# A macaron block with delta-rule attention on one core: the plain chunk inverses are stored ahead of the copy that turns them

## The reference

```
x = x + 0.5 * ffn(layernorm(x))      # 256 -> 1024, gelu, -> 256
x = x + attn(layernorm(x))
x = x + 0.5 * ffn(layernorm(x))

# attn, for each of 4 heads of 64:
q, k, v = silu(short_conv(x @ Wq)), silu(short_conv(x @ Wk)), silu(short_conv(x @ Wv))
beta = sigmoid(x @ Wb)
# delta rule, in chunks of 32 tokens (q, k normalised; kb = k * beta):
A = -tril(kb @ k.T, -1)
T = solve_triangular(eye - A, eye, lower=True)      # inverse of a unit lower triangle
u, w = T @ (v * beta), T @ kb
u_i = u - w @ S ;  o_i = q @ S + tril(q @ k.T) @ u_i ;  S = S + k.T @ u_i
# then: four branches (two FIR filters of v, o, v) mixed by a gate, rmsnorm, @ Wo
```

## Time and profile before

| | us |
|---|---|
| timed runs, median (lowest, highest) | 1264.2 (1264.02, 1264.72) |
| profiled execution, span | 1267.5 |
| TensorE products busy (share) | 1090.1 (86%) |
| TensorE weight loads busy | 813.0 (64%) |
| VectorE busy | 836.8 (66%) |
| ScalarE busy | 547.8 (43%) |
| GpSimd busy | 410.0 (32%) |
| chain that ended last, by engine | TensorE 55%, VectorE 24%, ScalarE 8%, "issue" 5%, SP 3%, GpSimd 3%, DMA 1% |

### The profile page before, as it was taken

How to read it: one execution, slowest core, us unless ns; L and a number is a source line. 1 busy time by engine, 2 the same in 40 slices (tenths; PEclk the granted TensorE clock), 3 DMA queues, 4 the chain that set the end, 5 groups by cost and what they waited for, 6 DMA issues and landing times.

```text
span 1267.5 us, 25615 instructions
## 1 busy us (share of the span) xinstructions
PE 1090.1 (86%) x10348; PEld 813.0 (64%) x10348; DVE 836.8 (66%) x1556; ACT 547.8 (43%) x957; POOL 410.0 (32%) x640
## 2 busy tenths in 40 slices
PE   3778499789988999889988997899988998887738
PEld 2663387368854886378845894388746885477427
DVE  5754247686678857875677757785687757873363
ACT  1145125543375435643375327443474337531322
POOL 8005500482007610482019500581018400770000
PEclk9869679799999999999999999899999999995768
DMA  5031101402040201402040204101040204010000
GB/s 148 1 80 39 32 1 34 85 1 50 18 92 10 41 9 36 82 1 49 18 100 1 49 2 95 23 18 33 18 101 1 50 1 91 10 31 20 1 0 17
DMA packets 80245, 47.19 MB, mean 37 GB/s; under 512 B 55808, under 2 KB 73728, under 8 KB 80128
## 3 DMA queue, kind: packets, MB, share of 16 engines
q1 hardware_dynamic: 80128, 45.56, 16.0%
HBM read 30.86 MB, written 14.68 MB: 36 GB/s over the span
## 4 chain that ended last, share of the span: by engine, by line
PE 55%; DVE 24%; ACT 8%; issue 5%; SPq 3%; POOL 3%; DMA 1%; DVEq 0%; ACTq 0%; POOLq 0%
PE psum L774 11%; PE psum L776 9%; PE psum L775 9%; DVE conv_acc L1351 5%; PE psum L805 4%; DVE arena L1582 3%; PE psum L963 3%; PE psum L948 2%; PE psum L982 2%; PE psum L987 2%; SPq L346 2%; ACT arena L577 2%; DVE h_hi L1330 2%; PE psum L1140 2%; PE psum L903 2%
## 5 line engine op out<-in xcount | busy, mean ns | idle before, releaser
L515 POOL TENSOR_TENSOR l_prod<-arena 64x30 f32<-64x30 f32 (+14 forms) x240 | 151.5, 631 | 631.3 <-DMA arena<-l_dram 613.1
L573 ACT ACTIVATE h_f<-psum,b_col 128x512 f32<-128x512 f32 x128 | 88.0, 688 | 226.7 <-PE psum L776 205.6
L774 PE MATMUL psum<-w_hi,h_hi 128*128 128x256 f32 x512 | 153.1, 299 | 14.5 <-DVE h_lo L1331 14.4
L519 POOL TENSOR_TENSOR arena<-arena,l_prod 64x30 f32<-64x30 f32 (+14 forms) x240 | 157.2, 655 | 18.8
L776 PE MATMUL psum<-w_hi,h_lo 128*128 128x256 f32 x512 | 146.1, 285 | 0.0
L775 PE MATMUL psum<-w_lo,h_hi 128*128 128x256 f32 x512 | 146.1, 285 | 0.0
L1069 PE MATMUL psum<-v_shift,fir_w 128*32 128x512 f32 x1152 | 136.6, 615 | 3.4 <-DMA v_shift<-v_dram 3.4
L1351 DVE SCALAR_TENSOR_TENSOR conv_acc<-psum,conv_col,conv_acc 128x511 f32<-128x511 f32 x144 | 107.8, 748 | 35.1 <-ACT conv_acc L598 23.3
L1330 DVE CAST h_hi<-h_f 128x512 fp32r<-128x512 f32 x128 | 80.4, 628 | 66.5 <-ACT h_f L573 39.8
L774 PE MATMUL psum<-xt_hi,w_hi 128*128 128x512 f32 x256 | 110.2, 431 | 14.9 <-DVE b_half L1444 7.0
L774 PEld LDWEIGHTS psum<-w_hi,h_hi 128*128 128x128 f32 x512 | 98.9, 193 | 22.5 <-DVE h_lo L1331 18.2
(11 more groups left out here) (231 smaller groups left out, 2268.7 us busy)
## 6 DMA issues: line engine op xcount, KB each, us to landing
x_in<-in_L_attn_x SPq DMA_DIRECT2D x8, 512.0 KB, 4.0
v_dram<-v_fm SPq DMA_DIRECT2D x8, 512.0 KB, 2.8
v_shift<-v_dram SPq DMA_DIRECT2D x8, 512.0 KB, 4.9
out<-x_tok SPq DMA_DIRECT2D x8, 512.0 KB, 2.9
v_shift<-v_dram SPq DMA_DIRECT2D x8, 511.0 KB, 6.9
v_shift<-v_dram SPq DMA_DIRECT2D x8, 510.0 KB, 9.1
v_shift<-v_dram SPq DMA_DIRECT2D x8, 509.0 KB, 11.7
arena<-in_L_ffn_w SPq DMA_DIRECT2D x2, 1024.0 KB, 7.2
```

Of the source, the lines that this page charges most:

```text
L515: pool.tensor_tensor(prod, l_inv[:, k + 1:, k:k + 1].broadcast_to(shape), l_inv[:, k:k + 1, 0:k].broadcast_to(shape), ALU.mult).then_inc(i ...
L519: pool.tensor_tensor(l_inv[:, k + 1:, 0:k], l_inv[:, k + 1:, 0:k], prod, ALU.add).then_inc(inverted, 1)
L573: act.activation(h_f[:, m % 2, :], bank, ACT.Gelu, bias=b1_col[:, m:m + 1]).then_inc(read, 1)
L774: pe.matmul(dst, a_hi, b_hi, start=first, stop=False, **kw)
```

## The change

The store of the plain inverses now waits for 61 counts of `inverted`, which is the memset, and is issued ahead of the wait for the 62nd, the turning copy. The turned inverses are stored behind that wait, with a semaphore of their own, `tt_stored`. Of the loads the six into `t_low` are issued first, behind `t_stored` and `fir_done`, then the four into `x_t`, behind `tt_stored`. Nothing is changed on the other engines, and number, size and form of the DMAs stay as they are.

```diff
-        t_stored, t_loaded = sem("t_stored"), sem("t_loaded")
+        t_stored, tt_stored, t_loaded = sem("t_stored"), sem("tt_stored"), sem("t_loaded")
...
+                    sp.wait_ge(inverted, INV_STEPS * j + INV_STEPS - 1)
+                    sp.dma_start(t_dram.rearrange("c u i j -> (c u) i j"), l_inv[:, :, :]).then_inc(t_stored, 16)
                     sp.wait_ge(inverted, INV_STEPS * j + INV_STEPS)
-                    sp.dma_start(tt_dram.rearrange("c u j i -> (c u) j i"), l_turned[:, :, :]).then_inc(t_stored, 16)
-                    sp.dma_start(t_dram.rearrange("c u i j -> (c u) i j"), l_inv[:, :, :]).then_inc(t_stored, 16)
-                    sp.wait_ge(t_stored, 32 * j + 32)
-                    for c in range(CPT):
-                        sp.dma_start(x_t[32 * c:32 * c + 32, :, 32 * c:32 * c + 32],
-                                     tt_dram[c].rearrange("u j i -> j u i")).then_inc(t_loaded, 16)
+                    sp.dma_start(tt_dram.rearrange("c u j i -> (c u) j i"), l_turned[:, :, :]).then_inc(tt_stored, 16)
+                    sp.wait_ge(t_stored, 16 * j + 16)
                     sp.wait_ge(fir_done, j + 1)
                     for c in range(CPT - 1):
                         col = CHUNK * (c % 2)
                         for g in range(2):
                             sp.dma_start(t_low[32 * c:32 * c + 32, g, :, col:col + CHUNK],
                                          t_dram[c, 8 * g:8 * g + 8].rearrange("u i j -> i u j")).then_inc(t_loaded, 16)
+                    sp.wait_ge(tt_stored, 16 * j + 16)
+                    for c in range(CPT):
+                        sp.dma_start(x_t[32 * c:32 * c + 32, :, 32 * c:32 * c + 32],
+                                     tt_dram[c].rearrange("u j i -> j u i")).then_inc(t_loaded, 16)
```

## The result

The changed kernel is faster, by about twice what was forecast: 1254.06 us median (1247.41 to 1258.99, 20 runs) against 1262.53 (1255.3 to 1270.15, 20 runs) of the kernel before, ratio 0.9939, 95% interval 0.9919 to 0.9959. The forecast was 1260.3 with a range of 1256.0 to 1263.8, so the time lies outside, and the gain of 8.5 us stands against 3.9. Single runs of one kernel scatter over 12 to 15 us, which the three runs of before that were known ahead of the prediction (1264.0 to 1264.7) did not show; they lay 1.7 us above the median of twenty. Over all runs in which the mean clock is known too, 121 of the kernel before and 42 of the changed one, the means are 1261.8 and 1254.7 us: 7.1 us, standard error 0.7.

The account below looks back on a forecast made before the run. Two of eight merges, head and tail, were taken to wait for loads behind the stores. Gains of 2.55 and 1.33 us, 3.9 together, off 1264.2 gave 1260.3, range 1256.0 to 1263.8.

Parts of the forecast that it names:

- the two waits: TensorE waiting for loads at the head's and the tail's first merge product: gains of 2.55 and 1.33 us, 3.9 together.
- I take 3.6 and keep 2.9: Plain store's landing in the head: 3.6 us taken from the profile, 2.9 kept as the bound if alone on the queues.
- The estimate of 2.6: Landing of the 256 KB plain store by the skill's formula, 2.6 us; by it the forecast would be 1259.3.
- The tail: Entry of the last pass: loads land before VectorE ends, TensorE starts about 0.2 us behind VectorE, gaining 1.33 us.
- My forecast lets that moment move along with the work: TensorE's return to full clock, 17 us after work begins behind the head, was taken to shift with the work.
- Rival B: Behind the head, the clock returns earlier, behind the first filler: 5.4 us less, 1254.9 in all; chance 0.10.
- C: The tail's 1.54 us wait is not the loads, so only the head gains: 1261.6; chance 0.07.
- D: A refill of TensorE's code falls into a burst of loads, costing up to 8.1 us: 1268.4; chance 0.07.
- E: Store waits for something behind the memset, or issues and landing limit anyway; about 1.0 us gained: 1263.2; chance 0.06.
- A: Behind the head, the clock comes back later in the program, costing 2.7 us; net gain 1.2: 1263.0; chance 0.17.

Follow-up runs that it names:

- e1: Kernel before with the plain store ahead of the copy but the loads in the old order: 11.9 us from memset to the head's first merge product.
- e2: Kernel before with both stores behind the copy, the plain one first, and the loads in the new order: 12.5 us from memset to the head's first merge product.
- e7: Kernel before with the new order of stores and loads in the six body passes alone: ratio 0.9996 (0.9966 to 1.0025).
- e14: Kernel before with the new order in the head and the last pass, the old one in the six body passes: ratio 0.9966, mean 1256.7 us.
- e16: The kernel before, unchanged, run once more for a third trace; the kernel before against itself measured 1.0008 (0.9978 to 1.0038).
- e13: The changed kernel, run a third time: ratio to the kernel before 0.9979 (0.9948 to 1.0009), mean 1257.4 us.
- e9: Kernel before with 128 products that nobody reads (256 instructions with weight loads) ahead of the first merge's wait: ratio 0.9996 (0.9972 to 1.0021).
- e6: Kernel before with the new order of stores and loads in the last pass alone: ratio 0.9985 (0.9957 to 1.0013).
- e5: Kernel before with 45 products that nobody reads ahead of the first merge's wait: ratio 0.9972 (0.9942 to 1.0001).

## Why the prediction was wrong

*The mechanism of the two waits was right.* The early store took the copy off the chain, the swapped loads were needed for it (`e1`, `e2`), the two waiting merges gained and the six others did not (`e7`, `e14`), the tail's wait passed to VectorE, and the plain store, the ten issues and a last landing became the head's limit.

*"I take 3.6 and keep 2.9": mis-sized.* The plain store lands in 2.9. I took the row's duration with its circumstances, the other store half a microsecond ahead of it on the queue, though the change takes just that away; the turned store's 2.9 was the row to go by. The shorter landing is worth 0.7, but the ten issues took 0.2 longer and the last landing 0.1, so the head gained 3.04 instead of 2.55. The estimate of 2.6 by the Trainium skill's DMA: Bandwidth & Descriptors (Anatomy of one DMA) was nearer than the row, and still short of 2.88.

*The tail: 1.33 forecast, 1.0 to 2.2 measured.* The stretch from the memset falls from 13.2 or 13.3 to 12.0 and 12.3 in two traces and to 11.1 in the others. I had 11.95 from one trace. In that trace the clock fell to half for a moment just ahead of the merge (the slice 1136 to 1140 has 0.66), and VectorE's last step came late; behind a wait for loads this cost nothing. In the changed kernel VectorE ends the wait, and it counts. In the thirteen traces of the table VectorE's last step ends 10.8 us behind the memset's start in the six where the clock stood at full there, and 11.7 to 12.0 us in the six where it fell. That the fall is the cause is likely but not shown: in the thirteenth, `e16`, the step is late (12.1) without it. `e13`, with such a fall, starts as I computed (its chain of waits):

```profile
1128.49 0.03 DVEq L1343
1128.52 0.25 issue
1128.76 1.22 PE psum L877 x63
```

*"My forecast lets that moment move along with the work": the step that failed.* It held the return of the clock at 17 us behind the head's merge, and so the cost of half clock there at what one trace had. The clock's return is not tied to a step of the program but differs from one execution to the next, between 4 and 17 us behind the same product, and the first interval goes with it: 145.8 to 147.5 us where it is under 6, 150.0 to 152.1 where it is 10 or more. By the two profiles this is 5.2 of the 11.8 us; by the means over all runs it is less, as worked out below. My 17.2 was one draw. Rival B, at 0.10, gave its place and its size rightly (behind the first filler, 4.8 us after L875, and 5.4 us off; the changed kernel's trace has 4.9 and 5.2). I gave it as an effect of a shorter wait, which the traces don't bear out; a distribution would have been right.

How much of the mean is clock? Time at half clock, worked out from each run's span and mean clock (span x 2 x (1 - mean clock)), is 190.3 us for the kernel before and 183.2 for the changed one. Within either kernel a microsecond at half clock goes with 0.29 us of time. At equal half-clock time the changed kernel is 5.0 us faster (standard error 0.4), about what the stretches show, 3.0 in the head and 1.0 to 2.2 in the tail; the 7.1 us less at half clock are the other 2.0. Some 3 of these 7.1 are only the idle stretch grown shorter, in which half clock costs nothing, so that the split may as well be 5.9 and 1.2. The 0.29 is a correlation and not a price that an experiment showed: `e9` had 181 us at half clock and a mean of 1262.0, no faster than the kernel before (most of the time that it saved at half clock lies in the idle stretch, where it costs nothing).

With this the 6.2 us between the forecast, 1260.3, and the median, 1254.06, can be split roughly: 1.7 the reference (see there), 1.1 the two waits (5.0 instead of 3.9), 2.0 the lower half-clock time, and 1.4 what these twenty runs have over all runs (8.5 and 7.1).

*What stays open* is whether the new order makes an early return more likely. It was early in 5 of 6 traces with the new order in the head, in 1 of 5 with the old one, and in one of the two with half of the change (`e1`, `e2`). Chance can do that, and the set with `e13` had no less half clock with the new order. Keeping TensorE busy before the merge did not secure it. So the waits' part of the gain is shown, and the cause of the rest stays open.

*The reference.* The range was built around 1264.2, the median of three runs within 0.7 us. Twenty runs gave 1262.5 with a spread of 15. Around that, the same 3.9 us would have been 1258.6, still 4.5 above the result.

*The rivals.* C falls: the tail's "issue" was the loads, and `e6`, which changes nothing else, shortens that stretch from 13.3 to 11.1. D and E didn't come: the two stalls stayed where they were, and the store is issued 0.18 behind the memset's start. A, a later return, cannot be told from the draw. (Two bounds of the prediction differ: the store's and the load's give 1260.7, and the forecast's chance is put on a range up to 1260.9. Nothing hangs on it.)

## What to carry to other kernels

When a step is taken from between a producer and its DMA, walk the chain again with the landing that the transfer has alone, not with the one it had in company, and look for what hid behind the old wait and will now show. Read order changes by stretches between two fixed events in the trace, such as from the memset to the first product here, which repeat within 0.6 us where whole times scatter by 15. And before a forecast of a few microseconds, ask how far TensorE's clock differs from run to run: three agreeing runs don't tell.

## What the runs showed of the hardware

- Two stores of 256 KB on one queue, issued 0.5 us apart: the first lands in 2.9 us, the second in 3.6 to 3.7, whichever tensor it is.
- The same program got its full clock back 4.3, 16.9 or 17.2 us after the same product in three executions.
- Stalls of TensorE of 5 to 8 us without a releaser are waits for its code: each of the 38 in the 18 traces holds one 16 KB transfer of the `instruction` queue and ends 1.2 to 1.6 us after it. The two of the kernel before stand in bursts of long v_shift loads.
- Adding 60 or 90 instructions to TensorE's stream moved such stalls to other passes and made three of two, for example one interval from 151.7 to 137.5 and another from 139.0 to 144.9 us in `e5`; adding 256 left them in their passes.
- A buffer that GpSimd copies (L531) can be stored by DMA at the same time: over eight passes the copy took 2.08 us in the median beside the store and 2.08 without it, the longest 2.39 and 2.23. The Trainium skill's Trainium Architecture — The Big Picture (What this means for kernel authors), which says that DMA and engine accesses of SBUF don't contend, agrees.
